# Couples of edge tiles, each tile gathered once, in the edge stage of a graph attention layer with a mixture of experts behind it

## What is computed

```python
xh = (x @ W).reshape(N, H, D)                 # x: layer-normed
e = leaky_relu(a_src[src] + a_dst[dst], 0.2)  # per edge and head
e = exp(e - m[dst]);  denom = segment_sum(e, dst)
out = segment_sum(xh[src] * (e / denom[dst])[:, :, None], dst) + bias
x = x + batchnorm(out) + layernorm(x)
x = x + top2_of_8_experts(layernorm(x))       # 256 -> 1024 -> 256, gelu
```

## Time and profile before

| | us |
|---|---|
| median of 3 runs (lowest, highest) | 2181.05 (2179.94, 2183.12) |
| profiled execution | 2179.96 |
| its span | 2178.0 |
| stage 1, to the first gather | 85.4 |
| edge stage, first gather to end of the last | 1365.0 as a stretch (85.4 to 1450.4) |
| edges' rest, batch-norm, experts | 727.6 |

### The profile page before, as it was taken

The page is one execution under the profiler, slowest core; times in us unless marked ns, Lnnn a source line. Parts: engine busy times, 40 slices in busy tenths (PEclk is TensorE's granted clock), DMA queues, the critical chain, the costliest instruction groups (busy, mean ns, idle before and its releaser), DMA issues. The chain is left out here.

```text
span 2178.0 us, 37746 instructions
## 1 busy us (share of the span) xinstructions
PE 1758.3 (81%) x10860; PEld 1227.8 (56%) x10860; DVE 1415.2 (65%) x3855; ACT 1108.1 (51%) x2386; POOL 1214.5 (56%) x1142
## 2 busy tenths in 40 slices
PE   7567778678777687687776887788399999999997
PEld 5334445354444354454443444447179999999996
DVE  6745666567666566566665676589956666666664
ACT  4444655465556456455654565548644444444443
POOL 1465655566656556566655566642046666656653
PEclk9778988888989889889998899899699999999999
DMA  8543444443444344344533444426723333333322
GB/s 292 168 123 95 123 108 116 116 136 97 121 138 123 96 130 126 97 125 122 146 93 108 133 127 108 118 61 229 292 64 51 51 51 51 50 51 51 51 43 36
DMA packets 124147, 240.42 MB, mean 110 GB/s; under 512 B 25064, under 2 KB 82996, under 8 KB 122772
## 3 DMA queue, kind: packets, MB, share of 16 engines
q0 software_dynamic: 62800, 147.76, 28.7%
q1 hardware_dynamic: 51816, 80.51, 11.2%
q10 hardware_dynamic: 9340, 9.73, 1.3%
HBM read 195.47 MB, written 43.30 MB: 110 GB/s over the span
## 5 line engine op out<-in xcount | busy, mean ns | idle before, releaser
L1145 POOL DMA_INDIRECT gather_ring<-node_table,src_slot x879 | 838.9, 954 | 530.8 <-issue 238.8
L1273 PE MATMUL bank<-gather_ring,onehot 128*128 128x264 f32 x1758 | 622.6, 439 | 262.0 <-DVE gather_ring L1197 222.0
L1239 PE MATMUL bank<-ones 128*128 128x512 bf16 x1803 | 595.0, 412 | 50.9 <-ACT gather_ring L1315 31.6
L1273 PEld LDWEIGHTS bank<-gather_ring,onehot 128*128 128x128 f32 x1758 | 340.2, 214 | 496.6 <-DVE gather_ring L1197 320.2
L1169 DVE TENSOR_TENSOR acc<-acc,bank 128x264 f32 x879 | 370.9, 422 | 192.5 <-remote 98.7
L1197 DVE TENSOR_TENSOR gather_ring<-gather_ring,bank 128x256 f32<-128x256 f32 x879 | 361.6, 412 | 0.3 <-ACT bank L1314 0.3
L1314 ACT ACTIVATE bank<-zbuf 128x64 f32<-128x64 f32 x110 | 25.0, 228 | 615.2 <-DVE zbuf L1191 346.5
L2240 POOL DMA_INDIRECT out_rows<-y,token_idx x105 | 203.6, 1939 | 218.4 <-DMA out_rows<-y,token_idx 151.7
L1239 PEld LDWEIGHTS bank<-ones 128*128 128x128 bf16 x1803 | 180.5, 104 | 208.4 <-issue 81.1
L2148 PE MATMUL bank<-xe,w_hi 128*128 128x256 f16 (+1 forms) x1792 | 284.2, 267 | 3.8 <-DVE xe L2070 2.6
L2208 ACT ACTIVATE hid<-bank,cols 128x256 f32<-128x256 f32 (+1 forms) x448 | 210.6, 551 | 150.7 <-PE bank L2148 137.3
(11 more groups left out here) (323 smaller groups left out, 1932.7 us busy)
## 6 DMA issues: line engine op xcount, KB each, us to landing
stage<-in_L_ffn_W SPq DMA_DIRECT2D x16, 1024.0 KB
dst_row<-dst_rows SPq DMA_DIRECT2D x110, 128.0 KB
gather_ring<-node_table,src_slot POOLq DMA_INDIRECT x879
w_split<-w_out SPq DMA_DIRECT2D x32, 256.0 KB
w<-w_split SPq DMA_DIRECT2D x8, 1024.0 KB, 9.9
node_table<-acc ACTq DMA_DIRECT2D x24, 264.0 KB
r_ring<-in_x_lanes SPq DMA_DIRECT2D x7, 896.0 KB, 8.0
xt<-in_x_lanes SPq DMA_DIRECT2D x24, 256.0 KB
```

Source lines behind the costliest of these rows:

```text
L1145: e.indirect_dma_start(out=gather_ring[:, b % GB, j, :], out_offset=None, in_=node_table, in_offset=bass.IndirectOffsetOnAxis(ap=src_slot[ ...
L1239: e.matmul(to[:, :].rearrange("p (k n) -> p k n", k=2), halves[:, 0:P], halves.rearrange("p (a n) -> p a n", a=1).broadcast_to([P, 2, 2 * ...
L1273: e.matmul(bank[AGG[s % len(AGG)]][:, 0:ROW], onehot[:, b % OHB, j, :], gather_ring[:, b % GB, j, :], start=True, stop=True).then_inc(summ ...
```

## The change

Two neighbouring edge tiles make a couple: CT = 416. A slot is now one couple with one node tile: USED = 416 + 49 - 1 = 464, SB = 4 slots in a batch, 116 batches. Gathers are no longer tied to slots: each edge tile is gathered once, 104 batches of 8 tiles, into the same ring of 4 batches. A slot finds its rows in the ring through a register. The messages, one operation of 128x512 per slot, go to a ring of their own (MR = 6 slots), which also takes the exponentials; the sum is two matmuls into one PSUM bank with one signal, and there is one addition per slot, ADDS_BEHIND = 2. GpSimd waits for `messages` up to a count from a table in registers, SyncE waits for the gather queues up to counts of the table and signals `rows_landed`, for which the score waits. The products of constants leave the edge stage. `onehot` keeps 2 batches. Tile numbers are loaded eight at a time for every second batch. In the lists' stage the destinations come by 4 indirect DMAs of 256 wide rows, the sources by one direct DMA and seven transposes, and VectorE makes the table of counts. The diff, cut to its core:

```diff
@@ -46 +46 @@
     NT = ceil_div(N, P)
     LAST = N - (NT - 1) * P
     ET = ceil_div(E, P)
-    SLOT_GROUPS = ceil_div(ET + NT, P)
+    TILE_GROUPS = ceil_div(ET, P)
+    COUPLE = 2
+    WIDE = COUPLE * P
+    CT = ceil_div(E, WIDE)
+    SLOT_GROUPS = ceil_div(CT + NT, P)
     SLOTS_UP = SLOT_GROUPS * P
     EB = 8
-    SLOTS = ceil_div(ET + NT - 1, EB) * EB
-    BATCHES = SLOTS // EB
-    USED = ET + NT - 1
+    SB = EB // COUPLE
+    USED = CT + NT - 1
+    SLOTS = ceil_div(USED, SB) * SB
+    BATCHES = SLOTS // SB
     ROW = D + HEADS
     PICK = 2 * HEADS
     TOP = 2
...
@@ -179 +181 @@
-        OHB = 3
+        MR = 6
+        message_ring = early.take("message_ring", [P, MR, COUPLE, ROW])
+        OHB = 2
         onehot = early.take("onehot", [P, OHB, EB, P])
         onehotT = early.take("onehotT", [P, 2, EB * P], BF16)
         dst_row = early.take("dst_row", [P, 2, EB * P], U8)
...
@@ -548 +575 @@
+                e.tensor_copy(slot_table[SPANS_AT:SPANS_AT + 32, 0:SLOT_GROUPS * PER_GROUP],
+                              bank[7][SPANS_AT:SPANS_AT + 32, P:P + SLOT_GROUPS * PER_GROUP]).then_inc(slot_keys_made, 1)
+                for h in range(2):
+                    hs = slice(h * HALF_SLOTS, (h + 1) * HALF_SLOTS)
+                    vector_order.of(e.tensor_copy(slot_table[landed, hs], bank[5 + h][landed, 0:HALF_SLOTS]))
+            if n == LISTS_AT + 4 + SLOT_GROUPS:
+                e.wait_ge(vector_order.sem, vector_order.n)
+                ends = slot_table[landed, 0:BATCHES * SB].rearrange("p (b q) -> p b q", q=SB)[:, :, SB - 1]
+                e.tensor_single_scalar(last_batch[landed, :], ends, 2, ALU.arith_shift_right).then_inc(slot_keys_made, 1)
+            thresholds = slot_table[landed, 0:BATCHES * GB].rearrange("p (b q) -> p b q", q=GB)
+            if n == LISTS_AT + 5 + SLOT_GROUPS:
+                e.wait_ge(slot_keys_made, ROWS_TAKEN)
+                for q in range(GB):
+                    vector_order.of(e.tensor_single_scalar(thresholds[:, :, q], last_batch[landed, :], GB - q, ALU.add))
+                e.wait_ge(vector_order.sem, vector_order.n)
+                vector_order.of(e.tensor_single_scalar(thresholds, thresholds, 2, ALU.arith_shift_right))
+            if n == LISTS_AT + 6 + SLOT_GROUPS:
+                e.wait_ge(vector_order.sem, vector_order.n)
+                e.tensor_scalar(thresholds, thresholds, 16 * EB, 16 * EB, ALU.mult, ALU.max).then_inc(slot_keys_made, 1)
...
@@ -872 +944 @@
         POOL_DIVIDES = GROUPS - 2
         dst_row_loaded = [sem(f"dst_row_loaded{i}") for i in range(2)]
         scalar_order = Order(sem("scalar_order"))
-        AGG, ADDS_BEHIND = (0, 1, 3, 4), 3
+        AGG, ADDS_BEHIND = (0, 1, 3, 4), 2
         PICKS = (2, 7)
-        idle_bank, IDLE_PRODUCTS = bank[5], 16
+        idle_bank = bank[5]
         gained = bank[6]
-        tile_regs = {}
+        tile_regs, landed_regs = {}, {}
+        SPANS_AT_ONCE = 8
 
         unit_loaded, bias_done = sem("unit_loaded"), sem("bias_done")
         max_made, max_turned, peaks_made, peaks_spread, unit_scaled = (
...
             return slice(g * NG, (g + 1) * NG)
 
         def slots_in(b):
-            return range(b * EB, min((b + 1) * EB, USED))
+            return range(b * SB, min((b + 1) * SB, USED))
 
         def final_at(g):
-            return ET + (g + 1) * NG - 1
+            return CT + (g + 1) * NG - 1
+
+        def load_row_of(e, row, at, n, least, most):
+            _, values = nc.values_load_multi_w_load_instructions(
+                slot_table[row:row + 1, at:at + n], engines=[e.engine], min_val=least, max_val=most,
+                skip_runtime_bounds_check_because=IN_RANGE)
+            return values
 
         def load_tiles(e, b):
-            _, values = nc.values_load_multi_w_load_instructions(
-                node_tile_row[0:1, b * EB:(b + 1) * EB], engines=[e.engine], min_val=0, max_val=NT,
-                skip_runtime_bounds_check_because=IN_RANGE)
-            tile_regs[e.engine, b] = values
+            if b % 2 == 0:
+                values = load_row_of(e, TILES_AT, b * SB, min(2, BATCHES - b) * SB, 0, NT)
+                tile_regs[e.engine, b], tile_regs[e.engine, b + 1] = values[0:SB], values[SB:]
+
+        def tiles_of(t):
+            return range(t * EB, (t + 1) * EB)
 
         def pool_first_edges(e):
+            e.wait_ge(src_kept, TILE_GROUPS)
             e.wait_ge(slots_kept, SLOTS_KEPT)
             e.wait_ge(slot_keys_made, KEYS_MADE)
             e.wait_ge(rows_written, 16 * SLOT_GROUPS)
@@ -1138,14 +1219,18 @@
             pool_edges(e, range(GB))
 
         def pool_edges(e, batches):
-            for b in batches:
-                if b >= GB:
-                    e.wait_ge(summed, (b - GB + 1) * EB)
-                for j, s in enumerate(slots_in(b)):
+            for t in batches:
+                if t >= GB:
+                    if (t - GB) % SPANS_AT_ONCE == 0:
+                        at = t - GB
+                        spans = load_row_of(e, SPANS_AT, at, min(SPANS_AT_ONCE, TILE_BATCHES - GB - at), 1, USED)
+                    e.wait_ge(messages, spans[(t - GB) % SPANS_AT_ONCE])
+                    e.sem_inc(m_sems["passed"], 1)
+                for j, i in enumerate(tiles_of(t)):
                     e.indirect_dma_start(
-                        out=gather_ring[:, b % GB, j, :], out_offset=None, in_=node_table,
-                        in_offset=bass.IndirectOffsetOnAxis(ap=src_slot[:, s:s + 1], axis=0)
-                    ).then_inc(gathered[b % GB], 16)
+                        out=gather_ring[:, t % GB, j, :], out_offset=None, in_=node_table,
+                        in_offset=bass.IndirectOffsetOnAxis(ap=src_tile[:, i:i + 1], axis=0)
+                    ).then_inc(gathered[t % GB], 16)
 
         def pick_bank(b):
             return bank[PICKS[b % 2]][:, 0:W_AT].rearrange("p (j i c) -> p j c i", i=3, c=PICK)
@@ -1161,7 +1246,7 @@
 
         def vector_edges(e):
             def add(b, j):
-                s = b * EB + j
+                s = b * SB + j
                 e.wait_ge(summed, s + 1)
                 if s:
                     e.wait_ge(added, s)
...
@@ -1174,13 +1259,19 @@
                 vector_order.of(e.tensor_reduce(picked[:, b % 2, :, :], pick_bank(b), AX.X, ALU.add))
                 vector_w1_bias(e, b)
 
+            def row_at(b, j):
+                return ring_rows[:, bass.ds((b * SB + j - tile_regs[e.engine, b][j]) % PLACES, 1), :, :]
+
             def score(b):
-                e.wait_ge(gathered[b % GB], 16 * (EB * (b // GB) + len(slots_in(b))))
+                e.wait_ge(rows_landed, GB * (b + 1))
                 e.wait_ge(vector_order.sem, vector_order.n)
                 if b:
                     e.wait_ge(weighed, 2 * b)
-                vector_order.of(e.tensor_tensor(zbuf[:, 0, :, :], gather_ring[:, b % GB, :, D:ROW],
-                                                picked[:, b % 2, :, 0:HEADS], ALU.add))
+                for j in range(len(slots_in(b))):
+                    of = slice(COUPLE * j, COUPLE * (j + 1))
+                    vector_order.of(e.tensor_tensor(zbuf[:, 0, of, :],
+                                                    row_at(b, j)[:, :, :, D:ROW].rearrange("p a r h -> p (a r) h"),
+                                                    picked[:, b % 2, of, 0:HEADS], ALU.add))
                 e.wait_ge(vector_order.sem, vector_order.n)
                 vector_order.of(e.scalar_tensor_tensor(zbuf[:, 1, :, :], zbuf[:, 0, :, :], NEG_SLOPE,
                                                        zbuf[:, 0, :, :], ALU.mult, ALU.max))
...
@@ -1191,18 +1282,24 @@
                 e.tensor_tensor(zbuf[:, 1, :, :], zbuf[:, 1, :, :], zbuf[:, 0, :, :], ALU.subtract).then_inc(scored, 1)
 
             def message(b, j):
-                row = gather_ring[:, b % GB, j, 0:D].rearrange("p (h d) -> p h d", d=DH)
+                s = b * SB + j
                 if j == 0:
                     e.wait_ge(weighed, 2 * b + 1)
-                e.tensor_tensor(row, row, weights(b)[:, j, :].rearrange("p (h a) -> p h a", a=1)
-                                .broadcast_to([P, HEADS, DH]), ALU.mult).then_inc(messages, 1)
+                if s >= MR:
+                    e.wait_ge(summed, s - MR + 1)
+                e.tensor_tensor(message_ring[:, s % MR, :, 0:D].rearrange("p r (h d) -> p r h d", d=DH),
+                                row_at(b, j)[:, :, :, 0:D].rearrange("p a r (h d) -> p (a r) h d", d=DH),
+                                weights(b)[:, COUPLE * j:COUPLE * (j + 1), :].rearrange("p r (h a) -> p r h a", a=1)
+                                .broadcast_to([P, COUPLE, HEADS, DH]), ALU.mult).then_inc(messages, 1)
 
...
             def messages_and_adds(b):
                 for j, s in enumerate(slots_in(b)):
                     message(b, j)
                     if s >= ADDS_BEHIND:
-                        add(*divmod(s - ADDS_BEHIND, EB))
-                    if j == EB // 2 - 1:
```

(71 more changed lines are left out.)

197 lines of the change are left out of this document (116 added, 81 removed).

## The result

The changed kernel takes 2289.45 us (median; 2286.87 to 2302.17), the kernel before 2182.09 beside it: a ratio of 1.0495, interval 1.0456 to 1.0535. Slower, where 2018 was forecast. But that is only half of the result. The kernel before takes 2182 us in this comparison and 2192 in a later set on chip 5; which chip the result came from is not known. On six other chips it takes 1901 to 1904. On two of these the changed kernel itself ran too, and took 1840 us, a ratio of 0.968. The cause of the loss is visible only where the kernel before takes 2182 or more. I call such a chip a pausing chip, the others even ones. No chip was seen in both conditions, and chip 10 was even in two sets; whether the condition belongs to the chip for good was not tested.

What follows compares the result with a forecast made beforehand. GpSimd's queue, work plus pauses, was taken to bound the edges: 2180.0 - 57.5 (fewer gathers) - (288.8 - 175) (shorter pauses) + 8 (register loads) = 2016.7, with the median's 1.1 2018 us. Forecast's own range 1873 to 2103; overall 1900 to 2195.

Steps and rivals of the forecast that it cites:

- The reading of the pauses: Edges: TensorE's signals are taken late while GpSimd gathers; GpSimd's work plus 288.8 us of pauses sets the length.
- I take 1.75: GpSimd's pause before each of 100 gather batches, in us: 175 us in all against 288.8; bounds 0.3 and 5.05.
- the late signal costs more than before: Edges, rival, chance 0.22: more VectorE work falls after late signals, two-batch gather runs grow; pause 3.7 us, total 2213.
- fewer signals in each run, and four batches of slack: Argument against longer pauses in the edges: fewer TensorE signals per gather run, and gathered rows buffered four batches deep.
- VectorE's loop: VectorE's work in the edges: 7.2 us per batch of four couples, 835 us over 116 batches, under GpSimd's 1020.
- Half clock: Edges, rival, chance 0.13: without products TensorE's clock falls and TensorE joins the loop, 11.4 us a batch, total 2138.
- Gathers with issue: GpSimd in the edges: 832 gathers in place of 879, 47 x 1.224 = 57.5 us less.
- Register loads on GpSimd: Edges: 13 loads of eight values at 0.6 us each, 8 us added uncovered, between 0 and 16.
- Lists: Stage before the first gather: fewer indirect loads, more TensorE and VectorE work; between -3 and +5 us, taken as 0.
- SyncE: Edges: VectorE's score waits for SyncE's count of landed gathers; 0 to 0.3 us per batch, hidden, so 0.
- Behind the last gather: End of the edges: some 26 us of work on four batches of rows, left as it is, within 4 us.
- ScalarE: ScalarE's work in the edges: 7.2 us per batch, 835 us in all, hidden under GpSimd.

Runs made afterwards that it cites:

- leave by sums: Changed kernel with GpSimd waiting for TensorE's sums, not VectorE's messages, before gathering: ratio 1.0616 (2325.4 us) on a pausing chip; 1840.2 and 1841.0 us on even ones.

## Why the prediction was wrong

*The reading of the pauses* stood in the main, for the chip of the result: GpSimd's queue sets the edges' length, and VectorE waits for TensorE's signals until a run of gathers is over. In the semaphore records of the changed kernel's trace, 72 of the 109 recorded picks' signals of the edges came more than 0.5 us after the latest pick, 6.6 us on average; on an even chip all 107 recorded ones came at once.

One thing the prediction did not say: the signals aren't late from the start of a run. Of the picks and sums that TensorE finished during the first two gathers of a run, 89% have a signal recorded within 0.1 us (77% in the kernel before), during the third 59% (65%), the fourth 34% (47%), the fifth 15% (15%), and from the sixth on 6% (4%); on an even chip it is 98% over the whole edges. The late ones mostly come 1.5 to 3.5 us after the run's last gather. So about 5 us at the head of each run are free, and what the loop doesn't get done in them is left for the pause.

*The step that failed* is "I take 1.75: two batches in three keep the 2.0 us pause of the usual one (1.33), and one in 25 the 10.1". It was 4.5 us a batch (451.7/100). A usual pause had 3.8 us, not 2.0, and double runs came 26 times in some 78 pauses, not 4 in 100. The prediction took the change to leave each pause as it was; in its place the runs showed that more of VectorE's work falls into it, 3.2 us behind the signal where it was 1.1. The sum with the measured pause is 2180.0 - 57.5 + (451.7 - 288.8) + 8 = 2293 before the smaller terms, against 2302.2 profiled. With those terms as measured (below; the register loads lie in the time of the gathers and their issue) it closes: 2180.0 - 36.1 + 162.9 - 7.3 + 2.4 + 0.4 = 2302.3.

*The rival "the late signal costs more than before"* named the mechanism and the point from which it decides (3.4), but gave it 3.7 and a chance of 0.22; its 2213 is 76 us short. Its mis-sized term is what is left of a run of eight: 0.46 couples, since the first 6 us would get some four, where 1.8 were left. I gave it too little because I argued with "fewer signals in each run, and four batches of slack". Neither helped. A second part of it fell: leave by messages in place of sums is not what makes double runs, since leave by sums had more of them.

*VectorE's loop.* Its busy time was right (793/116 = 6.8 us, forecast 7.2 with gaps), the time around the loop was not: 8.2 a batch, or 9.2 for eight gathers. A run of eight gathers lasts 10.0 (8 x 1.25). On an even chip 9.2 fits beneath it; where signals stop coming within a run, the part of the loop that needs them has to be done in the pause, and the traces show that part grown. Why it grew stays open. A longer loop is one candidate, but the loop of the kernel before was never run with cheap transfers: VectorE alone is busy 878.62/110 = 8.0 us there for eight gathers, so the loops differ by 1.2 us at most. Less slack (additions two behind in place of three, one-hots two batches ahead in place of three) would look the same.

*Half clock*: the clock did fall, from 0.87 to 0.70 over the edges (0.81 on an even chip), a mean of stretches at either level; the sums' matmuls took 531 ns a record in place of 439, with TensorE idle 758 us before them in place of 262, and nothing came of it on the even chips or, with the products back, on a pausing one. By the Trainium skill's rule ("TensorE: Matmul & The Clock Gate", "HAM oscillation") the array drops to half clock after idle stretches. The trace agrees (0.70 with the more idle TensorE), and the price stayed hidden, as forecast.

*Smaller terms.* Gathers with issue: 1040.0 us for 832, 1.250 each, so 36 saved in this pair of traces, not 57.5: the register loads lie in this time, and fewer gathers than before start behind a pause, which hides their 0.3 us of issue. On even chips it is the whole gain, 47 x 1.26 = 59 of some 60 us. Register loads on GpSimd: 13 with a median of 566 ns, as taken. Lists: the first gather at 78.1 in place of 85.4, 7.3 won, outside -3 to +5. SyncE: 1.7 us of the score's waits on the pausing chip, 91.5 on an even one, where GpSimd gathered on without pauses all the same. Behind the last gather: +2.4. ScalarE 778/116 = 6.7, forecast 7.2. Two slips in the prediction changed nothing: 288.8/106 is 2.7 us, not 2.8, and the weights' share of VectorE comes to 0.7 a batch, not 0.8. It also names two ranges, 1873 to 2103 and 1900 to 2195; the result lies outside both.

On an even chip neither kernel pauses, so only the term of the gathers is left of the forecast, and it came out: 1840 against 1902.

## What to carry to other kernels

Before a pause is priced, ask whether it belongs to the kernel or to the chip it ran on: one profile can't say, a second chip can, and here it turned a loss of 5% into a gain of 3%. Where a pause both costs time and lets held work through, split it at the signal that ends the hold: here, after a run of eight gathers, the wait for the signal was the same in both kernels, and the work behind it was what grew. A loop hidden under an issuing queue should be measured by itself, with that queue made cheap, before it is called hidden.

## What the runs showed of the hardware

The same program took 2182 and 2192 us in two sets and 1901 to 1904 on six other chips, 280 us less. On a pausing chip it isn't only TensorE's signals: single counts of SyncE take up to 1.4 us in place of 0.017. The long register loads are no such sign, since an even chip has them too, up to 1.1 us. The changed kernel on the result's chip, then on an even one:

```profile
L1449 SPq EVENT_SEMAPHORE  x464: 2/17/1384, 91.0 to 1572.7; - x155
...
L1200 SPq TENSOR_LOAD <-slot_table x56: 5/530/1293, 145.9 to 1549.7; - x56
L1200 POOLq TENSOR_LOAD <-slot_table x13: 323/566/1055, 105.6 to 1507.9; - x13
```
```profile
L1449 SPq EVENT_SEMAPHORE  x464: 17/17/17, 93.4 to 1133.4; - x155
...
L1200 SPq TENSOR_LOAD <-slot_table x56: 520/528/1098, 123.8 to 1110.0; - x56
L1200 POOLq TENSOR_LOAD <-slot_table x13: 321/565/584, 108.0 to 1071.0; - x13
```

VectorE's signals came at once in both: with VectorE's score done and ScalarE free, ScalarE's exponential started within 0.08 us in all 116 batches, and TensorE's sum within 0.41 us of its message in all 464 slots. ScalarE's recorded signals came at once too, but on the pausing chip not all signals are recorded (356 of the 464 of VectorE's messages, against 464 on the even one), so of ScalarE it is less sure. The stretch after the edges, which has indirect transfers too, is 700 us on the one and some 680 on the other. What a pausing chip has that the others haven't, no run here shows, nor whether it is the gathers' work on GpSimd or their transfers that hold the signals.
